# Where a batch's variances stand in VectorE's order: behind the last row maximum of the segment before

## The chip, the cores and the metric

One core of one Trainium2 chip. The metric is the device time of one execution in microseconds, the median of the runs, where lower is better.

## The reference

Two layers over `x` (4 batches x 512 rows x 256) and a context (4 x 1024 x 192). Each layer is a cross attention with 16 heads of 64 followed by a mixture-of-experts block; a layer normalisation without weights stands ahead of each. Cut to what matters here:

```python
def _layernorm(x, axis=-1, eps=1e-05):
    m = jnp.mean(x, axis=axis, keepdims=True)
    v = jnp.var(x, axis=axis, keepdims=True)
    return (x - m) / jnp.sqrt(v + eps)
...
    sim = jnp.einsum('bhid,bhjd->bhij', q, k) * SCALE
    attn = jax.nn.softmax(sim, axis=-1)
    out = jnp.einsum('bhij,bhjd->bhid', attn, v)
...
    x = x + _L0_xattn_ref(_layernorm(x, axis=-1), ctx_768, ...)
    x = x + _L0_ffn_ref(_layernorm(x, axis=-1), ...)
    x = x + _L1_xattn_ref(_layernorm(x, axis=-1), ctx_768, ...)
    x = x + _L1_ffn_ref(_layernorm(x, axis=-1), ...)
```

## The kernel before

The kernel runs four phases one after the other: attention and experts of layer 0, attention and experts of layer 1 (tile names begin with L0a, L0e, L1a, L1e and, for the sorted experts at the end, L1s). The change lies in the two attention phases. They are built by one function, `attention_phase`.

An attention phase is a software pipeline of 32 segments: 4 batches times 8 pairs of heads (`HP = 8`), segment `i` being head pair `i % 8` of batch `i // 8`. Every engine has its own written-out order of instructions for a segment, and the engines are tied by semaphores. In segment `i`

- TensorE transposes the last row maximum (L802), projects the queries of `i + 1`, and forms eight steps `qk(i, p)` of transposed scores (L818, L819), each step pair followed by a part of a value projection (`project_values`, L708); then it projects the output of `i - 1` (L708), and forms the scores of `i + 1` for their row maxima (L796), the products with the values (L833), the keys of `i + 2`, and the sums of the exponentials (L845);
- ScalarE takes the exponentials (L400) and the high parts of keys, weights and values (L381, L371, L375, L464);
- GpSimd (POOL) adds the exponentials over the keys (`psums`, L326), and forms low parts by a subtraction of two operands in SBUF: of the context (L334, in segments 0 and 1 of a batch), of the value weights (L312, in even segments) and of the attention weights (L307, in every segment);
- VectorE (DVE) works in the order `low_keys(i + 1, 1)` (L521, the low parts of the second half of the next keys, two instructions), the layer normalisation's piece of this segment if there is one, `normalise(i - 1)` (L535 reciprocal, L538), `high_output` and `low_output` (L544, L548), the queries' high and low parts (L504, L509), `add_output(i - 1)` (L558), and the four row maxima of `i + 1` (L530), with two instructions of L521 among them.

The normalisation of the batches next door is spread over the segments of a batch by `step = i % 8`: statistics in steps 0 and 1 (L566), the variances in step 2 (`ROOT`), then a square root on ScalarE behind its exponentials (L406), and the scales in steps 3 and 4. `variance` handles 4 or 8 columns (128x4 or 128x8). It issues six small instructions: L578, L579 and L580 follow one another with no wait between them, L581, L582 and L583 each stand behind a wait on a VectorE semaphore (`link`). All but L583 read two operands in SBUF.

A few other instructions that read two operands in SBUF come into the rows below: L624 (VectorE, segment 0) adds the bias to the residual; in the experts' phase L1087 (GpSimd) forms a chunk's low weights, L1181 (VectorE) forms low parts, L1208 follows it with no wait, and L1209 stands behind a wait on L1208's semaphore.

Two waits on TensorE look at VectorE here. In `project_values` the first part in an even segment waits for `low_keys(i + 1, 1)`, whose keys share its bank; the third part waits for `low_output(i - 1)`:

```python
elif n % 2 == 0:
    pe.wait_ge(sem["klo"], 2 * (i + 1) + 2)
...
else:
    pe.wait_ge(sem["olo"], i)
```

Of the kernel before, what the change touches and what calls it, by code (L numbers as in the profile page):

```python
# [46 lines left out]
def build(nc, x, ctx_top, ctx_bot, layer_in, out):  # L47
# [6 lines left out]
    with stack:  # L54
# [37 lines left out]
        def attention_phase(tag, weights, value_weights, bias, xres, prefetch, source=None, again=False, keep=False, clear=()):  # L92

            with scope() as s:
# [29 lines left out]
                with nc.Block() as block:  # L124
# [23 lines left out]
                    def half_of(n):  # L148
                        return slice(n * BANK, (n + 1) * BANK)

                    def bank_of_keys(i, half):
                        return bank(SPARE if i < 2 and half == 0 else PLACE[f"K{half}"])
# [10 lines left out]
                    NEXT_STATS, LAST_STATS, ROOT, INNER, OUTER, BIAS = 0, 1, 2, 3, 4, 7  # L163
# [17 lines left out]
                    def columns_of(b):  # L181

                        used = [column for _, column in batches_of(b)] if b >= 0 else [0]
                        return slice(min(used), max(used) + QT)
# [313 lines left out]
                    def _(dve):  # L498
# [15 lines left out]
                        def low_keys(i, n, heads=(0, 1)):  # L514
                            par, cols = i % 2, half_of(n)
                            if heads == (0,) and n == 0:
                                dve.wait_ge(sem["first_hi"], i + 1)
                            else:
                                dve.wait_ge(sem["hi"], 2 * i + n + 1)
                            for h in heads:  # L520
                                last = nc.vector.tensor_tensor(k_st[HEAD[1 - h], par, h, cols], bank_of_keys(i, n)[HEAD[h], :],  # L521
                                                               k_st[HEAD[h], par, h, cols], ALU.subtract)
                            if 1 in heads:
                                last.then_inc(sem["klo"], 1)
# [8 lines left out]
                        def normalise(i):  # L533
                            dve.wait_ge(sem["total"], i + 1)
                            nc.vector.reciprocal(inv[:, :], bank(PLACE["TOTAL"])).then_inc(sem["inv"], 1)  # L535
                            dve.wait_ge(sem["inv"], i + 1)
                            dve.wait_ge(sem["pv"], i + 1)
                            nc.vector.tensor_tensor(O, O, inv[:, :], ALU.mult).then_inc(sem["norm"], 1)  # L538
# [21 lines left out]
                        def statistics(b, step):  # L560

                            c, column = (b + 1, 0) if step == NEXT_STATS else (b - 1, QT)
                            if step == LAST_STATS:
                                dve.wait_ge(sem["added"], BEFORE + 2 * (b * HP - 1) + 2)
                            for t in range(QT):
                                nc.vector.bn_stats(stats[:, column + t, :], xres[:, c * QT + t, :]).then_inc(sem["stat"], 1)  # L566
                            dve.wait_ge(sem["stat"], counted_stats(b, step))
# [3 lines left out]
                        def link(b, n, ins):  # L571
                            ins.then_inc(sem["link"], 1)
                            dve.wait_ge(sem["link"], LINKS * (b + 1) + n)

                        def variance(b):
                            c = columns_of(b)
                            me, se, mo, so = (stats[:, c, i] for i in (1, 2, 4, 5))
                            nc.vector.tensor_tensor(total_of[:, c], me, mo, ALU.add).then_inc(sem["link"], 1)  # L578
                            nc.vector.tensor_tensor(var[:, c], se, so, ALU.add).then_inc(sem["link"], 1)  # L579
                            link(b, 3, nc.vector.tensor_tensor(dif[:, c], me, mo, ALU.subtract))  # L580
                            link(b, 4, nc.vector.scalar_tensor_tensor(dif[:, c], dif[:, c], DIM / 4.0, dif[:, c], ALU.mult, ALU.mult))  # L581
                            link(b, 5, nc.vector.tensor_tensor(var[:, c], var[:, c], dif[:, c], ALU.add))  # L582
                            nc.vector.tensor_scalar(var[:, c], var[:, c], 1.0 / DIM, EPS, ALU.mult, ALU.add).then_inc(sem["var"], 1)  # L583

                        def inner_scales(b):
                            c = columns_of(b)
                            dve.wait_ge(sem["sqrt"], b + 2)
                            if b > 0:
                                dve.wait_ge(sem["xn"], 2 * len([i for i in GROUPS if i <= b * HP + INNER]) + 2)
                            link(b, 6, nc.vector.reciprocal(rstd[:, c], std[:, c]))  # L590
                            link(b, 7, nc.vector.tensor_tensor(dif[:, c], var[:, c], rstd[:, c], ALU.mult))
                            link(b, 8, nc.vector.tensor_tensor(dif[:, c], dif[:, c], rstd[:, c], ALU.mult))

                        def outer_scales(b):
                            c = columns_of(b)
                            link(b, 9, nc.vector.tensor_scalar(dif[:, c], dif[:, c], -0.5, 1.5, ALU.mult, ALU.add))
                            link(b, 10, nc.vector.tensor_tensor(rstd[:, c], rstd[:, c], dif[:, c], ALU.mult))
                            link(b, 11, nc.vector.scalar_tensor_tensor(shift[:, c], total_of[:, c], -0.5, rstd[:, c], ALU.mult, ALU.mult))
                            dve.sem_inc(sem["scale"], 1)
# [17 lines left out]
                        def add_bias(b):  # L617
                            if b == 0:
                                dve.wait_ge(sem["bias"], 16)
                                dve.wait_ge(sem["xn"], 2)  # L620
                            else:
                                dve.wait_ge(sem["xn"], rows_of(b))
                            rows = xres[:, b * QT:(b + 1) * QT, :]
                            nc.vector.tensor_tensor(rows, rows, bias_sb[:, :].unsqueeze(1).broadcast_to([P, QT, DIM]), ALU.add)\  # L624
                                .then_inc(sem["biased"], 1)

                        def segment(i):
                            if i + 1 < SEGMENTS:
                                low_keys(i + 1, 1)
                            b, step = divmod(i, HP)  # L630
                            if step == NEXT_STATS and b + 1 < BATCH:
                                if b == 0 and source is not None:
                                    dve.wait_ge(sem["x1"], 16)
                                statistics(b, step)
                            if step == LAST_STATS and b > 0:
                                statistics(b, step)
                            if step == ROOT:
                                variance(b)
                            if step == INNER:
                                inner_scales(b)  # L640
                            if step == OUTER:
                                outer_scales(b)
                            if i == 0:
                                add_bias(0)
                            if step == BIAS and b + 1 < BATCH:
                                add_bias(b + 1)
                            if i > 0:
                                normalise(i - 1)
                            if i > 0:
                                high_output(i - 1)  # L650
                                low_output(i - 1)
                            if i + 1 < SEGMENTS:
                                high_queries(i + 1)
                                low_queries(i + 1)
                            if i > 0:
                                if i in GROUPS:
                                    low_rows(number(i), GROUPS[i][0], PLACE["XT"])
                                add_output(i - 1)
                            if i + 1 < SEGMENTS:
                                for qt in range(QT):  # L660
                                    maximum(i + 1, qt)
                                    if qt in (1, 2) and i + 2 < SEGMENTS:
                                        low_keys(i + 2, 0, (qt - 1,))

                        nc.vector.memset(row_max[:, QT - 1, :], 0.0).then_inc(sem["pad"], 1)
                        if source is not None:
# [1097 lines left out]
```

## Time and profile before

| | before |
|---|---|
| median of 3 runs | 2612.82 us (2611.64 to 2613.31) |
| profiled execution, its own time | 2618.82 us |
| its span | 2616.9 us |
| granted TensorE clock, mean over the span | 0.985 |
| TensorE matmul busy | 96% |
| VectorE busy | 80% |
| GpSimd busy | 57% |
| ScalarE busy | 48% |

The profiled execution took 6.0 us more than the median of the timed ones; the span leaves out 1.9 us of it. Positions in the rows below are microseconds from the start of the span.

### The profile page before, as it was taken

Reading aid. Unit: us, or ns where it says so; the run is one execution under the profiler, and the core shown is the slowest. Engines: PE = TensorE matmul, PEld = TensorE weight load, DVE = VectorE, ACT = ScalarE, POOL = GpSimd, SP = SyncE. Lnnn points to the kernel's source line nnn. Section 1 sums busy time; section 2 is a strip of 40 time slices with the busy share of each in tenths; the row PEclk is TensorE's granted clock in tenths of the full one; section 3 lists DMA queues with packets and bytes.
Section 4 is the critical chain, followed back from the end, with each engine's and each line's share of the span. In section 5 each row is a group of like instructions: output and inputs, shape, how many; then the busy total and the mean of one; then the engine's idle time right before and its main releaser. Section 6 shows DMA issues by size and latency. Waiting matters only on the chain. (4 is left out here: it accounts for less than half of the span.)

```text
span 2616.9 us, 37958 instructions
## 1 busy us (share of the span) xinstructions
PE 2520.7 (96%) x13304; PEld 1776.5 (68%) x13304; DVE 2091.2 (80%) x2602; ACT 1246.1 (48%) x1774; POOL 1482.1 (57%) x1124
## 2 busy tenths in 40 slices
PE   8999999999999889999999899999999999998795
PEld 6666565656665678888888766666666665656684
DVE  7888888888888487777777788888888888866695
ACT  5555555555554323333333355455555454533393
POOL 5878777877777311111111187687878777760345
PEclk9999999999999999999999999999999999999897
DMA  4122212222221200000000121222131222115112
GB/s 147 45 59 53 63 45 58 63 49 50 63 51 41 72 19 24 24 24 24 24 24 18 47 75 45 55 61 59 45 79 45 59 53 55 45 29 235 47 54 88
DMA packets 118648, 145.09 MB, mean 55 GB/s; under 512 B 63856, under 2 KB 80112, under 8 KB 117488
## 3 DMA queue, kind: packets, MB, share of 16 engines
q1 hardware_dynamic: 113664, 136.10, 19.3%
q0 software_dynamic: 1536, 4.20, 0.5%
q10 hardware_dynamic: 3312, 3.02, 0.3%
q8 instruction: 81, 1.33, 0.2%
q14 instruction: 55, 0.45, 0.1%
HBM read 80.93 MB, written 11.80 MB: 35 GB/s over the span
## 5 line engine op out<-in xcount | busy, mean ns | idle before, releaser
L326 POOL TENSOR_TENSOR L1a_psums<-L1a_psums,L1a_probs 128x512 f32<-128x512 f32 x384 | 479.1, 1293 | 0.0
L326 POOL TENSOR_TENSOR L0a_psums<-L0a_psums,L0a_probs 128x512 f32<-128x512 f32 x384 | 478.8, 1289 | 0.0
L530 DVE TENSOR_REDUCE L1a_row_max<-psum 128x2 f32<-128x2048 f32 x128 | 293.6, 2293 | 59.2 <-PE psum L796 58.9
L530 DVE TENSOR_REDUCE L0a_row_max<-psum 128x2 f32<-128x2048 f32 x128 | 293.5, 2293 | 57.7 <-PE psum L796 57.2
L400 ACT ACTIVATE L0a_probs<-psum 128x1024 f32<-128x1024 f32 x256 | 251.6, 1027 | 105.9 <-PE psum L819 105.7
L400 ACT ACTIVATE L1a_probs<-psum 128x1024 f32<-128x1024 f32 x256 | 251.6, 1027 | 105.1 <-PE psum L819 104.9
L1168 DVE SCALAR_TENSOR_TENSOR xres<-psum,L0e_weights_of,xres 128x256 f32<-128x256 f32 x544 | 225.6, 478 | 22.6 <-PE psum L1379 21.7
L833 PE MATMUL psum<-L1a_probs,L1a_v 128*64 128x512 f32 x1024 | 240.5, 601 | 0.0
L833 PE MATMUL psum<-L0a_probs,L0a_v 128*64 128x512 f32 x1024 | 240.4, 601 | 0.0
L1365 PE MATMUL psum<-xnT_hi,L0e_w_hi 128*128 128x512 f32 x544 | 215.0, 395 | 9.4 <-DVE L0e_hid L1176 9.4
L1365 PE MATMUL psum<-xnT_lo,L0e_w_hi 128*128 128x512 f32 x544 | 214.6, 394 | 0.0
L1365 PE MATMUL psum<-xnT_hi,L0e_w_lo 128*128 128x512 f32 x544 | 213.1, 392 | 0.0
L818 PE MATMUL psum<-L0a_q_hh,L0a_k_st 128*128 128x512 f32 x512 | 204.4, 399 | 1.4 <-ACT L0a_probs L400 0.9
L818 PE MATMUL psum<-L1a_q_hh,L1a_k_st 128*128 128x512 f32 x512 | 204.3, 399 | 1.4 <-ACT L1a_probs L400 0.9
L819 PE MATMUL psum<-L1a_q_lm,L1a_k_hs 65*128 65x512 f32 x512 | 203.1, 397 | 0.0
L819 PE MATMUL psum<-L0a_q_lm,L0a_k_hs 65*128 65x512 f32 x512 | 203.0, 397 | 0.0
L1113 ACT ACTIVATE L0e_act_g<-psum 128x512 f32<-128x512 f32 x136 | 81.3, 598 | 243.4 <-PE psum L1365 243.4
L558 DVE TENSOR_TENSOR xres<-psum,xres 128x512 f32<-128x512 f32 x128 | 88.6, 692 | 114.9 <-PE psum L708 113.8
L1176 DVE TENSOR_TENSOR L0e_hid<-psum,L0e_act_g 128x512 f32<-128x512 f32 x136 | 93.7, 689 | 102.8 <-ACT L0e_act_g L1113 102.7
L326 POOL TENSOR_TENSOR L1a_psums<-L1a_probs 128x512 f32<-128x512 f32 x64 | 82.4, 1307 | 153.5 <-ACT L1a_probs L400 153.5
L1087 POOL TENSOR_TENSOR L0e_w_lo<-L0e_raw,L0e_w_hi 128x768 fp32r<-128x768 f32 x16 | 30.0, 1875 | 242.1 <-ACT L0e_w_hi L1102 242.1
L1087 POOL TENSOR_TENSOR L0e_w_lo<-ctx_stage,L0e_w_hi 128x768 fp32r<-128x768 f32 x16 | 30.6, 1914 | 240.9 <-ACT L0e_w_hi L1102 240.9
(384 smaller groups left out, 6148.6 us busy)
## 6 DMA issues: line engine op xcount, KB each, us to landing
L0a_k_hs<-L0a_k_st SPq DMA_DIRECT2D x64, 256.0 KB, 3.6
L1a_k_hs<-L1a_k_st SPq DMA_DIRECT2D x64, 256.0 KB, 3.7
L0a_raw<-in_attention SPq DMA_DIRECT2D x33, 384.0 KB, 3.4
L1a_raw<-in_attention SPq DMA_DIRECT2D x33, 384.0 KB, 3.4
L1weights<-in_sorted SPq DMA_DIRECT2D x2, 6144.0 KB, 20.6
L0a_q_hh<-L0a_q_hh SPq DMA_DIRECT2D x64, 128.0 KB, 2.3
L1a_q_hh<-L1a_q_hh SPq DMA_DIRECT2D x64, 128.0 KB, 2.3
ctx_stage<-in_experts SPq DMA_DIRECT2D x19, 384.0 KB, 3.0
```

The lines of the kernel that those rows point to most:

```text
L326: nc.gpsimd.tensor_tensor(psums[:, h, :], a, probs[:, h, kv, :], ALU.add).then_inc(sem["acc"], 1)
L400: nc.scalar.activation(probs[:, h, 2 * kp:2 * kp + 2, :], slot(h).rearrange("p (n q) -> p n q", n=2), ACT.Exp, scale=SCALE)\
L530: nc.vector.reduce_max(row_max[:, qt, 0:33:32], psum[:, 0:4 * BANK].rearrange("p (h k) -> p h k", h=2), axis=AX.X).then_inc(sem["max"], 1)
L558: nc.vector.tensor_tensor(rows, bank(PLACE[f"OUT{half}"]), rows, ALU.add).then_inc(sem["added"], 1)
L818: nc.tensor.matmul(dst, k_st[:, par, h, keys_of], q_hh[:, par, h, :], start=True, stop=False)
L819: last = nc.tensor.matmul(dst, k_hs[0:DH + 1, par, h, keys_of], q_lm[0:DH + 1, par, h, :], start=False, stop=True)
L833: last = nc.tensor.matmul(O[HEAD[h], :], v[:, pair % 2, kv, cols], probs[:, h, kv, :], start=kv == 0, stop=kv == KVT - 1)
L1087: nc.gpsimd.tensor_tensor(w_lo[:, par, :], raw[par], w_hi[:, par, :], ALU.subtract)\
L1113: nc.scalar.activation(act_g[:, u % 2, :], bank(u % 2), ACT.Silu).then_inc(sem["silu"], 1)
L1168: last = nc.vector.scalar_tensor_tensor(acc, bank(4 + 2 * (u % 2) + n // 2)[:, (n % 2) * DIM:(n % 2 + 1) * DIM], weights_of[:, ds(j * (2 * ...
L1176: nc.vector.tensor_tensor(hid[:, u % 2, :], bank(2 + u % 2), act_g[:, u % 2, :], ALU.mult)\
L1365: last = nc.tensor.matmul(bank(2 * g + u % 2), a[:, par, w], m[:, kd, rows], start=n == 0, stop=n == 3 * KD - 1)
```

## The change

The call of `variance(b)` is moved up in VectorE's order: from segment `8b + 2`, where it stood behind the low keys (L521) and ahead of the reciprocal (L535), to the end of segment `8b + 1`, behind the fourth row maximum (L530) and so ahead of those low keys. Nothing else moves, no wait is added or taken away, and no other engine's order changes. The variances of the first batch before the pipeline starts, `variance(-1)`, stay where they are.

```diff
@@ -634,8 +634,6 @@
                                 statistics(b, step)
                             if step == LAST_STATS and b > 0:
                                 statistics(b, step)
-                            if step == ROOT:
-                                variance(b)
                             if step == INNER:
                                 inner_scales(b)
                             if step == OUTER:
@@ -661,6 +659,8 @@
                                     maximum(i + 1, qt)
                                     if qt in (1, 2) and i + 2 < SEGMENTS:
                                         low_keys(i + 2, 0, (qt - 1,))
+                            if step + 1 == ROOT:
+                                variance(b)
```

## Rows read from the trace of the kernel before

**Rows 1.** The page's first part: busy time, share of span, instructions.

```profile
PE 2520.7 (96%) x13304; PEld 1776.5 (68%) x13304; DVE 2091.2 (80%) x2602; ACT 1246.1 (48%) x1774; POOL 1482.1 (57%) x1124
```

**Rows 2.** Windows: seven segments with variances, first, last, sum; then the segments before.

```profile
86.00:113.00 27.00, 26.50 (x136) 16.32 (x134) 23.50 (x25) 15.55 (x21) 21.86 (x17) 1.00 0.26 65
...
1984.42:2011.49 27.07, 26.51 (x136) 16.30 (x134) 23.57 (x25) 15.56 (x21) 21.93 (x17) 1.00 0.26 65
sum 189.30, PE 185.60 PEld 114.20 DVE 164.79 ACT 108.91 POOL 153.26; mean PE 26.51 PEld 16.32 DVE 23.54 ACT 15.56 POOL 21.89
...
sum 183.67, PE 183.67 PEld 114.57 DVE 156.74 ACT 98.39 POOL 148.44; mean PE 26.24 PEld 16.37 DVE 22.39 ACT 14.06 POOL 21.21
```

**Rows 3.** Timeline of VectorE: start, duration, instruction; layer 0, segment 10.

```profile
294.94 2.29 DVE L530 TENSOR_REDUCE L0a_row_max<-psum 128x2 f32<-128x2048 f32 x1 [0.37 <-PE psum L796]
297.26 1.39 DVE L521 TENSOR_TENSOR L0a_k_st<-psum,L0a_k_st 64x512 fp32r<-64x512 f32 x2
298.69 1.49 DVE L578 TENSOR_TENSOR L0a_total_of<-L0a_stats 128x8 f32<-128x8 f32 x1
...
300.18 0.16 DVE L580 TENSOR_TENSOR L0a_dif<-L0a_stats 128x8 f32<-128x8 f32 x1
300.37 0.17 DVE L581 SCALAR_TENSOR_TENSOR L0a_dif<-L0a_dif 128x8 f32<-128x8 f32 x1
...
300.98 3.36 DVE L535 RECIPROCAL L0a_inv<-psum 128x512 f32<-128x512 f32 x1
...
305.83 0.69 DVE L548 TENSOR_TENSOR L0a_o_split<-psum,L0a_o_split 128x512 fp32r<-128x512 f32 x1
```

**Rows 4.** Timeline of GpSimd around the same place, and its next L307.

```profile
297.07 1.28 POOL L312 TENSOR_TENSOR L0a_wv<-L0a_raw_v,L0a_wv 128x512 fp32r<-128x512 f32 x1
298.30 1.84 POOL L307 TENSOR_TENSOR L0a_w_split<-L0a_raw,L0a_w_split 128x768 fp32r<-128x768 f32 x1
301.32 1.29 POOL L326 TENSOR_TENSOR L0a_psums<-L0a_probs 128x512 f32<-128x512 f32 x1 [1.17 <-ACT L0a_probs L400]
...
320.18 1.82 POOL L307 TENSOR_TENSOR L0a_w_split<-L0a_raw,L0a_w_split 128x768 fp32r<-128x768 f32 x1 [1.39 <-ACT L0a_w_split L371]
```

**Rows 5.** Timeline of TensorE and its weight loads in the same segment.

```profile
300.72 0.42 PEld L708 LDWEIGHTS psum<-L0a_wv,ctx_hi 128*128 128x128 f32 x2
...
305.65 0.39 PE L819 MATMUL psum<-L0a_q_lm,L0a_k_hs 65*128 65x512 f32 x1
...
306.58 0.30 PEld L708 LDWEIGHTS psum<-L0a_wv,ctx_hi 128*128 128x128 f32 x2 [0.97 <-DVE L0a_o_split L548]
```

**Rows 6.** The eighth place (layer 1, segment 26): VectorE, GpSimd and the window.

```profile
2198.03 0.17 DVE L578 TENSOR_TENSOR L1a_total_of<-L1a_stats 128x4 f32<-128x4 f32 x1
...
2198.97 3.36 DVE L535 RECIPROCAL L1a_inv<-psum 128x512 f32<-128x512 f32 x1
...
2194.20 1.82 POOL L307 TENSOR_TENSOR L1a_w_split<-L1a_raw,L1a_w_split 128x768 fp32r<-128x768 f32 x1
...
2196.90:2223.14 26.24, 26.24 (x135) 16.38 (x133) 22.20 (x25) 15.57 (x21) 19.31 (x15) 1.00 0.24 58
```

**Rows 7.** Timeline, segment 0 of layer 0: a VectorE instruction behind GpSimd's.

```profile
38.00 1.29 POOL L326 TENSOR_TENSOR L0a_psums<-L0a_probs 128x512 f32<-128x512 f32 x1 [1.71 <-ACT L0a_probs L400]
...
39.24 2.27 POOL L326 TENSOR_TENSOR L0a_psums<-L0a_probs 128x512 f32<-128x512 f32 x1
...
38.47 1.90 DVE L624 TENSOR_TENSOR xres<-xres,L0a_bias_sb 128x1024 f32<-128x1024 f32 x1
```

**Rows 8.** Timeline, experts of layer 0: a GpSimd instruction behind VectorE's.

```profile
929.69 2.98 POOL L1087 TENSOR_TENSOR L0e_w_lo<-ctx_stage,L0e_w_hi 128x768 fp32r<-128x768 f32 x1 [19.34 <-ACT L0e_w_hi L1102]
...
929.69 0.69 DVE L1181 TENSOR_TENSOR L0e_hid_lo<-L0e_hid,L0e_hid_hi 128x512 fp32r<-128x512 f32 x1
930.29 0.69 DVE L1208 TENSOR_TENSOR L0e_gt<-L0e_choice,L0e_late 128x512 f32<-128x512 f32 x1
931.02 2.20 DVE L1209 TENSOR_TENSOR L0e_eq<-L0e_choice,L0e_late 128x512 f32<-128x512 f32 x1
```

## The prediction

> **What bounds the kernel now.** The page's first part comes first: TensorE's matmuls are busy 96% of the span [rows 1]. So an edit on VectorE counts only where TensorE waits for VectorE. For that I cut the attention phases into segments at TensorE's transpose of the last row maximum and asked for windows. Seven of the eight segments that hold the variances last 27.00 to 27.13 us, 189.30 us in sum; the seven segments just ahead of them last 183.67 us in sum [rows 2]. The difference, 5.63 us or 0.80 us a segment, is what the variances cost now. It is also the most that moving them can give back.
>
> VectorE's timeline of one such segment shows how it comes about [rows 3]. From the variances' first instruction to the reciprocal they take 300.98 − 298.69 = 2.29 us, of which L578 alone is 1.49 us, though it has 8 columns. At the eighth place the same instruction takes 0.17 us and the whole 0.94 us [rows 6]. GpSimd's timeline tells them apart [rows 4, 6]: in the seven, L307 runs from 298.30 to 300.14 and L578 ends 0.04 us behind it, at 300.18; in the eighth L307 was over at 2196.02, 2.0 us ahead of L578. L578 and L307 both read two operands in SBUF, and VectorE stands until GpSimd is done.
>
> Last comes TensorE's timeline [rows 5]. Its last L819 ahead of the value projection starts at 305.65, and the next weight load only at 306.58, released by L548, which ends at 306.52 [rows 3]. That is the stall. Where the variances took 0.94 us the segment lasted 26.24 us, with no stall [rows 6]. So what counts is when L535, and with it L548, comes: 2.29 us of variances cost 0.80 us, the first 1.49 us are free.
>
> **The change, part by part.** The six instructions remain and nothing is waited for anew, but they stand 1.43 us earlier (L521 to L578 now, 297.26 to 298.69 [rows 3]), and GpSimd is then inside another pair of instructions. Their price at the new place is no row of the trace. I work it out at the segment of rows 3; the other six repeat it within a few hundredths.
>
> *Removed:* 2.29 us between L521 and L535.
>
> *Added ahead of L521:* L530 ends at 294.94 + 2.29 = 297.23. L578 has no wait in front of it, so it is issued between 297.15 (with no wait between, L1208 started 0.09 us before L1181 ended [rows 8]) and 297.26. GpSimd's L312 runs from 297.07 to 298.35, and L307 is queued right behind it, from 298.30 [rows 4]. I need to know who gets through when both queue.
> - A VectorE instruction that waits behind one of GpSimd's goes ahead of GpSimd's next. L624 was issued at 38.47 inside L326 (38.00 to 39.29) and ended at 40.37; the second L326, issued at 39.24, took 2.27 us for the 1.29 us of the first [rows 7]. So L578 goes ahead of L307 and ends 0.04 us behind L312, at 298.39.
> - VectorE instructions with no wait between them keep GpSimd out, and a wait between them lets it in. L1181 and L1208 ran back to back, 929.69 to 930.98, while L1087 stood; L1087 then ended at 932.67, 1.69 us after them, and L1209, behind a wait of only 0.04 us, took 2.20 us for the 0.69 us of L1208 [rows 8]. L579 and L580 have no wait in front, L581 has one. So L580 ends 0.16 us after L578 (as now, 300.34 after 300.18 [rows 3]), at 298.55, and then L307 goes in. It has the shape of L1087 and ends 1.69 us later, at 300.24.
> - L581 ends 0.04 us behind it, at 300.28. GpSimd has nothing more queued, since its L326 waits for the exponentials until 301.32 [rows 4]. From the end of L581 to the next instruction is 0.44 us (300.54 to 300.98 [rows 3]): L521 starts at 300.72.
>
> So VectorE spends 300.72 − 297.26 = 3.46 us on the variances and not 2.29. Behind them L521 and its gap take 1.43 us as before, and L535 starts at 302.15 where it started at 300.98: 1.17 us later. The move carries the chain across one GpSimd instruction more: it waits for the rest of L312, and then for all of L307 in its middle.
>
> *What is late next.* L521 now ends near 302.11. The value projection behind it would load its weights at 300.72 [rows 5], so TensorE stands there for about 1.4 us, a stall that did not exist (L521 ended at 298.65, 2.1 us early). With this it reaches the second wait about 1.3 us later, while L548 ends 1.17 us later, at 307.69: it stands there again, about half a microsecond in place of 0.93. Both waits hang on one VectorE chain, so they don't add: the segment ends later by the shift of L548 alone, 1.17 us.
>
> *What hides the rest.* GpSimd's L312 and L307 end up to 0.1 us later; the 1.17 us of idle time behind them covers it [rows 4]. Its next additions need the exponentials behind the first stall and slip by 1.3 us; they had 1.39 us to spare before the next L307, whose own input also comes later with TensorE [rows 4]. The square root is taken at the end of ScalarE's segment, so variances ready earlier or later are worth nothing there. No DMA waits for the low keys.
>
> *The eighth place:* GpSimd is idle, the variances take 0.94 us again, L521 ends 0.94 us later inside its 2.1 us of slack: nothing.
>
> *The sum:* 7 × 1.17 = 8.2 us. Both ends of the unknown, the order of access: if L307 went ahead of L578, L578 would end at 300.18 and L521 start at 300.98, 1.43 us late, 10.0 us in all; if L578, issued at 297.15, got in before L312 (issued only 0.08 us ahead of it), L312 would end near 298.6, L307 near 300.4 with L582 behind it, and L521 would start near 300.67: 1.12 us, 7.8 us in all. On the profiled execution's own time: 2618.8 + 8.2 = 2627.0, a factor of 1.0031; on the median, 2612.8 × 1.0031 = **2621.0 us**.
>
> The Trainium skill (SBUF — State Buffer, Who interferes with whom) says the shared port pair is an exclusive lock for the whole instruction, and that issue order decides who blocks. The rows agree that one side stands entirely. Taken to the letter, issue order would put L307 (298.30) ahead of L579 (298.31), which rows 8 speak against; it is the second rival.
>
> **Rivals.**
> 1. *VectorE keeps the access through its short waits* (not slower). The waits between L580 and L583 are 0.03 us each; if GpSimd doesn't get in there, the chain ends 298.39 − 300.18 + 300.98 = 299.19, L535 starts at 300.62, 0.36 us earlier than now, and the stall shrinks to 0.44 us a segment: −2.5 us, 2610.3. It decides wherever L307 can't start within a gap of 0.03 us. For it: L307 is one instruction's processing away from running. Against it: L1087 got in at a gap of 0.04 us [rows 8]. The floor under it, with all stalls gone, is −5.6 us, 2607.2 [rows 2]. Chance 0.12 with the floor.
> 2. *GpSimd's queued L307 goes in earlier.* Ahead of L579, L307 ends at 298.39 + 1.69 = 300.08, and L579 to L583 follow as now: L521 at 300.84, 1.29 us late, 9.0 us, 2621.8. Ahead of L578: 10.0 us, 2622.8. For it: L307 starts 0.05 us before L312 ends, back to back. Against it: rows 7, where the second L326 did the same and lost. Chance 0.10.
> 3. *The shift is taken up by slack I don't see,* as the statistics of steps 0 and 1 are in their segments (26.24 us on average just ahead [rows 2]): under 4 us, near 2615. Against it: beyond 1.49 us every tenth of the variances showed in the segment now. Chance 0.05.
>
> **How the numbers follow.** The forecast (7.8 to 8.2 us, either order at L312) has 0.73; its own range is 2619 to 2623, from the 1.7 us between the runs of before. With rival 2 it is 0.83, which reaches to 2622.8 and with the same spread to 2625. At the low end a shift of half a microsecond a segment, partly covered, gives 2616.5. Range 2616.5 to 2625. A measurement of this kernel tells 0.2%, 5.2 us, from no change. The forecast and rival 2 lie over it; of their 0.83 I give 0.05 to a time just under it. Rivals 1 and 3 are within it, but for 0.03 at the floor. Faster 0.03, same 0.19, slower 0.78.
>
> **What would show it.** Right: L578 of about 1.1 to 1.2 us right behind L530, L581 (or L582) of about 1.7 to 1.9 us, L307 of about 2 us on GpSimd; TensorE's weight load at the first part of the value projection released by L521, 1.4 us late; seven segments of 28.2 us and the eighth of 26.24. Wrong: L581 and L582 at 0.17 us each with L307 pushed behind L583, and segments of 26.7; or L578 at 2.9 us, with the order of rival 2. What would make it wrong altogether is a GpSimd that starts L312 somewhere else than some 0.1 us ahead of L578.

## The result, and the profile after

The changed kernel takes 2620.76 us (median of 8 runs, 2616.93 to 2621.79), the kernel before 2612.28 us (8 runs, 2611.32 to 2614.47): a ratio of 1.0029 with a 95% interval of 1.0018 to 1.0040. The medians lie 8.5 us apart, the ratio makes it 7.6 us. The kernel is slower, by an amount that the measurement can tell from nothing.

The windows after, cut like [rows 2] at the transpose of the last row maximum (start:end and length, then busy time and instructions of TensorE, its weight loads, VectorE, ScalarE and GpSimd, the granted clock, DMA's share and GB/s). The first of the seven is shown, then the eighth place, and the sum is that of the seven:

```profile
86.48:114.77 28.29, 26.74 (x135) 16.25 (x133) 24.80 (x25) 15.54 (x21) 21.89 (x17) 1.00 0.24 62
...
2206.56:2232.80 26.24, 26.24 (x135) 16.38 (x134) 22.20 (x23) 15.56 (x21) 19.31 (x15) 1.00 0.24 58
...
sum 198.13, PE 187.19 PEld 113.65 DVE 173.69 ACT 108.74 POOL 153.35; mean PE 26.74 PEld 16.24 DVE 24.81 ACT 15.53 POOL 21.91
```

The seven segments last 198.13 us where they lasted 189.30 [rows 2]: 8.83 us more, 1.26 us each. The eighth has 26.24 us as before [rows 6]. Every other segment of the two attention phases lasts as long in both kernels to within 0.05 us (26.1 to 26.7 us, the last one 25.4), so all of the difference that the attention phases make is in the seven. The granted clock is 1.00 in them, TensorE's upper level of 2.4 GHz, so the clock has no part in it.

VectorE's timeline in the segment of [rows 3] shows what they are made of (start, duration, instruction, then idle time before it with its releaser):

```profile
296.71 2.29 DVE L530 TENSOR_REDUCE L0a_row_max<-psum 128x2 f32<-128x2048 f32 x1 [0.37 <-PE psum L796]
299.04 1.11 DVE L578 TENSOR_TENSOR L0a_total_of<-L0a_stats 128x8 f32<-128x8 f32 x1
300.07 0.16 DVE L579 TENSOR_TENSOR L0a_var<-L0a_stats 128x8 f32<-128x8 f32 x1
300.15 1.82 DVE L580 TENSOR_TENSOR L0a_dif<-L0a_stats 128x8 f32<-128x8 f32 x1
302.01 0.17 DVE L581 SCALAR_TENSOR_TENSOR L0a_dif<-L0a_dif 128x8 f32<-128x8 f32 x1
...
302.61 1.39 DVE L521 TENSOR_TENSOR L0a_k_st<-psum,L0a_k_st 64x512 fp32r<-64x512 f32 x2
304.03 3.36 DVE L535 RECIPROCAL L0a_inv<-psum 128x512 f32<-128x512 f32 x1
...
308.88 0.69 DVE L548 TENSOR_TENSOR L0a_o_split<-psum,L0a_o_split 128x512 fp32r<-128x512 f32 x1
```

And GpSimd's, in the same place:

```profile
298.84 1.28 POOL L312 TENSOR_TENSOR L0a_wv<-L0a_raw_v,L0a_wv 128x512 fp32r<-128x512 f32 x1
300.08 1.87 POOL L307 TENSOR_TENSOR L0a_w_split<-L0a_raw,L0a_w_split 128x768 fp32r<-128x768 f32 x1
303.09 2.51 POOL L326 TENSOR_TENSOR L0a_psums<-L0a_probs 128x512 f32<-128x512 f32 x2 [1.15 <-ACT L0a_probs L400]
307.06 14.97 POOL L326 TENSOR_TENSOR L0a_psums<-L0a_psums,L0a_probs 128x512 f32<-128x512 f32 x12 [1.46 <-ACT L0a_probs L400]
323.19 1.82 POOL L307 TENSOR_TENSOR L0a_w_split<-L0a_raw,L0a_w_split 128x768 fp32r<-128x768 f32 x1 [1.16 <-ACT L0a_w_split L371]
```

Read the ends against each other. L312 ends at 300.12 and L578 at 300.15. L307 ends at 301.95 and L580 at 301.97. Two of the six instructions stand until the GpSimd instruction beside them is over; the other four take 0.16 or 0.17 us. The other six places repeat this within 0.02 us. From L578's start to L521's it is 302.61 − 299.04 = 3.57 us. Before, the six took 2.29 us in their old place [rows 3]. TensorE's timeline shows who pays:

```profile
304.15 0.47 PE L708 MATMUL psum<-L0a_wv,ctx_hi 128*128 128x256 f32 x2 [1.27 <-DVE L0a_k_st L521]
...
309.63 0.51 PE L708 MATMUL psum<-L0a_wv,ctx_hi 128*128 128x256 f32 x2 [0.32 <-DVE L0a_o_split L548]
...
304.12 0.30 PEld L708 LDWEIGHTS psum<-L0a_wv,ctx_hi 128*128 128x128 f32 x2 [1.67 <-issue]
...
309.63 0.30 PEld L708 LDWEIGHTS psum<-L0a_wv,ctx_hi 128*128 128x128 f32 x2 [0.74 <-DVE L0a_o_split L548]
```

Before there was one stall in the segment, behind L548 [rows 5]. Now there is one behind L521 first, and the old one is shorter. Behind L521 the trace names L521 at the matmul only; at the weight load, which waits 1.67 us, it names no releaser ("issue"). The trace's list of waits (engine and line, released by, us in total, times, longest) has the new one in all seven segments, four in layer 0 and three in layer 1:

```profile
PE psum L708 <- DVE L0a_k_st L521: 5.0, 4, 1.3
...
PE psum L708 <- DVE L1a_k_st L521: 3.8, 3, 1.3
```

### The profile page after: what moved, and what is told of

It reads as the page before. It is cut to its first block and busy times, and to the rows that moved or that the text cites. A ratio compares the mean times of both kernels' runs of the same rounds, so it can differ in the third digit from the quotient of the medians.

```text
span 2619.1 us, 37958 instructions
## 1 busy us (share of the span) xinstructions
PE 2516.0 (96%) x13304; PEld 1771.1 (68%) x13304; DVE 2100.4 (80%) x2602; ACT 1246.0 (48%) x1774; POOL 1482.4 (57%) x1124
## 5 line engine op out<-in xcount | busy, mean ns | idle before, releaser
L326 POOL TENSOR_TENSOR L0a_psums<-L0a_psums,L0a_probs 128x512 f32<-128x512 f32 x384 | 478.9, 1289 | 5.8 <-ACT L0a_probs L400 5.8
L326 POOL TENSOR_TENSOR L1a_psums<-L1a_psums,L1a_probs 128x512 f32<-128x512 f32 x384 | 478.9, 1289 | 4.3 <-ACT L1a_probs L400 4.3
L530 DVE TENSOR_REDUCE L0a_row_max<-psum 128x2 f32<-128x2048 f32 x128 | 293.6, 2293 | 57.7 <-PE psum L796 57.4
L530 DVE TENSOR_REDUCE L1a_row_max<-psum 128x2 f32<-128x2048 f32 x128 | 293.5, 2293 | 57.7 <-PE psum L796 57.4
L326 POOL TENSOR_TENSOR L1a_psums<-L1a_probs 128x512 f32<-128x512 f32 x64 | 82.3, 1305 | 153.5 <-ACT L1a_probs L400 153.5
```

Of the source, the lines that this page charges most:

```text
L326: nc.gpsimd.tensor_tensor(psums[:, h, :], a, probs[:, h, kv, :], ALU.add).then_inc(sem["acc"], 1)
L530: nc.vector.reduce_max(row_max[:, qt, 0:33:32], psum[:, 0:4 * BANK].rearrange("p (h k) -> p h k", h=2), axis=AX.X).then_inc(sem["max"], 1)
```

## The experiments

Theory A: the whole price, before and after, is waiting for GpSimd. L578 waits for L312, one more of the six waits for L307, and without these waits the place of the variances costs nothing. Theory B: the new place has a price of its own, since it puts the six ahead of the low keys, L521, for which TensorE's value projection waits. Two questions on the order of access were still open too: who goes first when both engines queue, and whether all GpSimd work is alike.

Of each run, the ratio is to the kernel before, run beside it, whose median was 2615.67 us (30 runs) beside experiments 1 to 4 and 2613.11 us (15 runs) beside 5 and 6. So a ratio or a count of segments can be compared between runs, a bare time can't. "Segments" is the length of the seven segments in its profile, and their excess is the sum over 7 × 26.24 = 183.68 us. By that count the kernel before has 5.6 us of excess and the changed one 14.4.

| kernel | ratio (95% interval) | segments, us | excess, us | less before's 5.6, us | by the ratio, us |
|---|---|---|---|---|---|
| the changed kernel | 1.0029 (1.0018 to 1.0040) | 28.28 to 28.32 | 14.4 | +8.8 | +7.6 |
| 1: GpSimd behind the variances | 0.9974 (0.9963 to 0.9984) | 26.24 | 0.0 | −5.6 | −6.8 |
| 2: only L307 behind them | 0.9986 (0.9977 to 0.9995) | 26.62 to 26.67 | 2.8 | −2.8 | −3.7 |
| 3: split between both places | 0.9996 (0.9987 to 1.0005) | 26.86 to 26.90 | 4.5 | −1.1 | −1.0 |
| 4: old place, segment 3 | 0.9983 (0.9974 to 0.9992) | 26.24 | 0.0 | −5.6 | −4.4 |
| 5: old place, GpSimd behind | 0.9980 (0.9971 to 0.9989) | 26.47 to 26.53 | 2.0 | −3.6 | −5.2 |
| 6: under the additions | 1.0231 (1.0215 to 1.0247) | 32.3 to 37.5 (all eight) | 66.5 | +60.9 | +60.4 |

(The last column is the ratio less one times 2612 to 2616 us. Runs 5 and 6 have something at the eighth place as well; it is in their excess.) The last two columns differ by 1.6 us at most, which is inside every interval. The segments leave out the rest of the program, which no version changes: what lies outside the two attention phases took between 970.0 and 976.6 us in the eight profiled executions. So the segments can be read finer than the medians, and what a version is worth is what its segments say.

**1. GpSimd's two instructions held until the variances are done.** Against the changed kernel. The place of the change stays; L312 and L307 can't be beside the six.

```
 def segment(i):
+    if i % HP == ROOT:
+        pool.wait_ge(sem["var"], i // HP + 2)
     if i % 2 == 0 and i // 2 + 1 < PAIRS:
         low_values(i // 2 + 1)
```

> The changed order, with GpSimd told to wait for the variances before its L312 and L307 of that segment (one wait more, in segments 8b+2). Theory A (the price is GpSimd's access, not the place): no variance instruction is held up, the six take 0.94 us as at the eighth place, which is under the 1.49 us that are free; L312 then runs from about 1.0 us after the last row maximum, L307 ends just ahead of the next L326, and all seven segments last 26.24 us: 5.6 us under before, near 2606.7, and 14 us under the changed kernel. Theory B (the place ahead of the low keys costs, whoever uses the access): the low keys are still behind the variances, TensorE still stands at the value projection, and the time stays above before, 2615 to 2620.

Measured: 2608.60 us (8 runs), ratio 0.9974. VectorE in the same segment (L580 to L585 are the changed kernel's L578 to L583, L523 its L521):

```profile
296.29 0.17 DVE L580 TENSOR_TENSOR L0a_total_of<-L0a_stats 128x8 f32<-128x8 f32 x1
296.38 0.17 DVE L581 TENSOR_TENSOR L0a_var<-L0a_stats 128x8 f32<-128x8 f32 x1
...
297.27 1.39 DVE L523 TENSOR_TENSOR L0a_k_st<-psum,L0a_k_st 64x512 fp32r<-64x512 f32 x2
```

The six take 0.98 us in place of 3.57, in the same place on VectorE, and the windows of all seven segments are those of a segment with nothing in it:

```profile
296.58:322.82 26.24, 26.24 (x135) 16.38 (x133) 22.23 (x23) 15.57 (x21) 22.35 (x17) 1.00 0.26 68
...
sum 183.69, PE 183.69 PEld 114.65 DVE 155.54 ACT 109.00 POOL 156.37; mean PE 26.24 PEld 16.38 DVE 22.22 ACT 15.57 POOL 22.34
```

TensorE is busy in every microsecond of them. So the 14.4 us of the changed kernel are waits for GpSimd and nothing else. For the 5.6 us of the kernel before, whose six stand in another place, it takes experiments 4 and 5. GpSimd's L328 (the L326 of before) now starts with no idle time at 300.44: the delay used up its 1.15 us of spare time and cost nothing more.

**2. Only L307 held.** The same wait, placed between `low_values` and `low_weights`: L312 stays beside the six.

> As the run before, but only L307 waits for the variances; L312 stays where it is. Theory A: L578 is held up by L312 (1.1 us) and nothing behind it is; the six take 1.9 to 2.0 us in place of 3.57, the segments last 26.7 us, 2.5 us under before, near 2609.8. So L312 would be worth 0.4 us and L307 1.6 us a segment. Theory B: as in the run before, 2615 to 2620.

Measured: 2611.75 us (11 runs), ratio 0.9986.

```profile
295.54 1.10 DVE L580 TENSOR_TENSOR L0a_total_of<-L0a_stats 128x8 f32<-128x8 f32 x1
296.56 0.16 DVE L581 TENSOR_TENSOR L0a_var<-L0a_stats 128x8 f32<-128x8 f32 x1
296.64 0.17 DVE L582 TENSOR_TENSOR L0a_dif<-L0a_stats 128x8 f32<-128x8 f32 x1
...
297.45 1.39 DVE L523 TENSOR_TENSOR L0a_k_st<-psum,L0a_k_st 64x512 fp32r<-64x512 f32 x2
```

L578's wait for L312 is still there, 1.10 us, and the instruction that took 1.82 us takes 0.17. Of the 14.4 us, L312 alone makes 2.8 (0.40 us a segment), and L307 adds the other 11.6 (1.66 us). The 1.65 us by which L580 is longer than 0.17 reach the end whole, since L312's delay has used up the free time. The shares hold in this order only: the free time goes to whichever delay is counted first, and no run has L307 beside the six in the new place without L312.

**3. Split.** Against the kernel before: part 0 of `variance` is L578 and L579, in the new place; part 1 is the other four, in the old one. L307 then runs beside L521, which reads PSUM and one operand in SBUF.

```
 if step == ROOT:
-    variance(b)
+    variance(b, 1)
...
+if step + 1 == ROOT:
+    variance(b, 0)
```

> Only L578 and L579 at the new place, the other four at the old one, behind the low keys L521, which have one operand in SBUF. Theory A: L578 takes 1.1 us behind L312, L307 runs under L521, and L580 is held up for only 0.3 us: L535 comes 0.1 to 0.2 us earlier than before, segments 26.9 us, near 2611.3. Theory B: the low keys are late by 1.2 us of their 2.1 us of slack and VectorE does the same work: about as before or, if the low keys' lateness costs in proportion, 2615.

Measured: 2613.53 us (11 runs), ratio 0.9996, which can't be told from the kernel before; segments 26.86 to 26.90 us against its 27.00 to 27.13. GpSimd's instruction and VectorE's stand here one below the other (L579 and L580 are the changed kernel's L578 and L579, and L583 is its L580):

```profile
297.63 1.87 POOL L307 TENSOR_TENSOR L0a_w_split<-L0a_raw,L0a_w_split 128x768 fp32r<-128x768 f32 x1
...
296.60 1.10 DVE L579 TENSOR_TENSOR L0a_total_of<-L0a_stats 128x8 f32<-128x8 f32 x1
297.62 0.16 DVE L580 TENSOR_TENSOR L0a_var<-L0a_stats 128x8 f32<-128x8 f32 x1
297.81 1.39 DVE L521 TENSOR_TENSOR L0a_k_st<-psum,L0a_k_st 64x512 fp32r<-64x512 f32 x2
299.24 0.29 DVE L583 TENSOR_TENSOR L0a_dif<-L0a_stats 128x8 f32<-128x8 f32 x1
```

L521 takes its usual 1.39 us under L307: it isn't held. Only the last 0.26 us of L307 (to 299.50) meet an instruction with two operands in SBUF, and that one takes 0.29 us in place of 0.17. The waits are a matter of which instruction lies beside which, not of GpSimd being busy. From L579 to L521 the first two and their gap take 1.21 us (296.60 to 297.81) and the other four 0.93 us (299.24 to 300.17), 2.14 us in all.

**4. The old place, one segment later.** The kernel before with `ROOT` 3 in place of 2, and the inner scales moved from step 3 to 4. GpSimd prepares value weights in even segments alone, and its L307 there is over before the six come.

> The kernel before with ROOT = 3 and INNER = OUTER = 4: the variances behind the low keys of segment 8b+3, the square root at the end of that segment, and both pieces of the scales in segment 8b+4. GpSimd has nothing to run there (its L307 is over 3 us ahead and the next additions come 2 us later). Theory A: variances 0.94 us, scales about 1.3 us, both under the 1.49 us that are free: all segments 26.24 us, near 2606.7. Theory B says nothing of this place. A third possibility is that the scales in one piece (six instructions, 1.2 to 1.3 us) go over the free time and give back some tenths a segment, 2608 to 2610.

Measured: 2609.99 us (11 runs), ratio 0.9983. All segments last 26.24 us, and the six take 0.16 to 0.17 us each. The scales in one piece take 1.35 us (353.12 to 354.47), less than the 1.49 us that are free, so the third possibility didn't come about either. The same 5.6 us come back without a wait on GpSimd. That speaks against theory B's counterpart as well: the old place isn't bad either, only what lay beside it.

**5. The old place with experiment 1's wait.** If the new place has no price of its own, this is as fast as experiment 1.

> The order of before (variances behind the low keys), with GpSimd told to wait for them ahead of L312 and L307, as in e1_pool_after_var. Theory A (access alone): the variances take 0.94 us here too, all segments last 26.24 us, 5.6 us under before, the same as e1_pool_after_var. GpSimd's additions start 1.5 us later than before and have 1.4 us to spare, so at most 0.1 us a segment could come back. Theory B (the place ahead of the low keys has a price of its own): this one is faster than e1_pool_after_var.

Measured: 2608.20 us (11 runs), ratio 0.9980. The variances are uncontended, 0.98 us from L580's start to the reciprocal's, but the segments last 26.47 to 26.53 us, and 26.42 at the eighth place. TensorE's weight loads name the cause:

```profile
300.37 0.30 PEld L710 LDWEIGHTS psum<-L0a_wv,ctx_hi 128*128 128x128 f32 x2 [0.43 <-POOL L0a_wv L312]
```

and GpSimd's rows the rest:

```profile
299.03 1.29 POOL L312 TENSOR_TENSOR L0a_wv<-L0a_raw_v,L0a_wv 128x512 fp32r<-128x512 f32 x1 [2.76 <-issue]
300.28 1.84 POOL L307 TENSOR_TENSOR L0a_w_split<-L0a_raw,L0a_w_split 128x768 fp32r<-128x768 f32 x1
```

L312 makes the low value weights that the value projection loads. Held behind the variances of the old place it ends at 300.32, and TensorE wants them some 0.4 us earlier. In experiment 1 L312 starts 0.79 us into its segment (297.37 − 296.58) and here 2.22 us (299.03 − 296.81), so there it is over in time. The expectation said that at most 0.1 us a segment would be left; it was 0.23 to 0.29, and 0.18 at the eighth place. It missed a user of GpSimd's result that isn't GpSimd. By segments the new place is better than the old by 2.0 us once GpSimd waits, and the medians can't tell them apart. Theory B is refuted: the place that it blames is the better one.

**6. The six under GpSimd's long series.** Against the kernel before. The variances moved to the segment ahead, behind the low queries and ahead of `add_output`, where GpSimd runs twelve of its additions, L326, back to back. It asks what the order of access does when GpSimd never pauses.

```
-    if step == ROOT:
-        variance(b)
...
         high_queries(i + 1)
         low_queries(i + 1)
+    if step + 1 == ROOT:
+        variance(b)
     if i > 0:
```

> The variances in segment 8b+1 ahead of add_output (L558), where VectorE is idle for 1.4 us but GpSimd runs its additions L326 back to back, one every 1.25 us. Theory A with what the changed kernel showed (a queued GpSimd instruction goes in behind the second variance instruction and then at every wait): L578 is held up by the rest of one L326, and L580, L581 and L582 each by a whole one; the six take about 4.5 us, L558 comes 3 us late in all eight places, and the 5.6 us of before are given back: plus 18 us, near 2631; if L583, with one operand in SBUF, is held up as well, plus 28 us, near 2641. The weaker reading (GpSimd gets in once for the whole group): the six take 2.6 us, L558 is 1.1 us late, plus 3 us, near 2615. Theory B: TensorE doesn't wait for anything here, and the idle time hides them: 2607.

Measured: 2672.71 us (4 runs), ratio 1.0231, far over both expectations. VectorE, at the segment of the rows above and at the next place:

```profile
287.53 0.45 DVE L578 TENSOR_TENSOR L0a_total_of<-L0a_stats 128x8 f32<-128x8 f32 x1
287.91 1.33 DVE L579 TENSOR_TENSOR L0a_var<-L0a_stats 128x8 f32<-128x8 f32 x1
289.16 1.31 DVE L580 TENSOR_TENSOR L0a_dif<-L0a_stats 128x8 f32<-128x8 f32 x1
290.50 1.18 DVE L581 SCALAR_TENSOR_TENSOR L0a_dif<-L0a_dif 128x8 f32<-128x8 f32 x1
291.72 1.19 DVE L582 TENSOR_TENSOR L0a_var<-L0a_var,L0a_dif 128x8 f32<-128x8 f32 x1
292.94 1.19 DVE L583 TENSOR_SCALAR L0a_var<-L0a_var 128x8 f32<-128x8 f32 x1
...
506.76 10.29 DVE L578 TENSOR_TENSOR L0a_total_of<-L0a_stats 128x8 f32<-128x8 f32 x1
```

```profile
282.91 14.86 POOL L326 TENSOR_TENSOR L0a_psums<-L0a_psums,L0a_probs 128x512 f32<-128x512 f32 x12
...
502.14 14.88 POOL L326 TENSOR_TENSOR L0a_psums<-L0a_psums,L0a_probs 128x512 f32<-128x512 f32 x12
```

In the first case L578 waits for the rest of one addition and each of the other five for a whole one, 1.2 to 1.3 us, with or without a wait of its own in front: 6.6 us for what takes 0.94 alone. In the second L578 is let in only when the series ends (517.02; L578 ends at 517.05), having waited through the rest of one addition and all of the next eight. That happened at two of the eight places (the other is 2231.02, 10.28 us). At a third, L578 took 2.95 us, the rest of one and two more; at the other five it took 0.45 to 0.65 us. GpSimd's series takes 14.86 and 14.88 us for its twelve, against 14.97 without the six beside it (the changed kernel's row above), so VectorE pays all of it.

The delay costs TensorE more than its own length. It waits for the first row maximum behind the six, and then runs for a while at a lower clock:

```profile
297.71 1.22 PE L796 MATMUL psum<-L0a_k_st,L0a_q_hh 64*128 64x512 f32 x4 [4.71 <-DVE L0a_row_max L530]
```

```profile
276.65:310.46 33.81, 29.10 (x136) 18.10 (x134) 29.14 (x29) 14.05 (x19) 21.36 (x17) 0.90 0.19 50
298.00:304.00 6.00, 6.00 (x16) 3.85 (x16) 2.98 (x2) 1.65 (x3) 0.00 (x0) 0.50 0.07 3
304.00:308.00 4.00, 4.00 (x22) 1.27 (x20) 3.15 (x3) 3.02 (x5) 0.80 (x1) 1.00 0.52 131
```

The stall ends at 297.71. The granted clock (third number from the end) is 0.50 of full speed from 298 to 304, the lower of the two levels, 1.2 GHz, and 1.00 again from 304 on. Over the segment it is 0.90, where the same segment has 1.00 in the kernel before and in the changed one. Of the 33.81 − 26.24 = 7.57 us that this segment lost, 4.71 are the stall. The other 2.9 us agree with TensorE's busy time, which is 2.86 us more than the 26.24 of a full segment for as many instructions. The windows of all eight segments, added up, say the same:

```profile
sum 276.38, PE 229.69 PEld 143.09 DVE 242.09 ACT 111.44 POOL 169.25; mean PE 28.71 PEld 17.89 DVE 30.26 ACT 13.93 POOL 21.16
```

They lost 66.5 us, of which 276.38 − 229.69 = 46.7 us are stalls, and 229.69 − 8 × 26.24 = 19.8 us are matmuls that took longer. The granted clock is 0.86 to 0.90 in each of the eight.

## Why the prediction was right

Forecast were 2621.0 us and a shift of 8.2 us; measured were 2620.76 and 8.5 between medians, 8.8 by segments. The sign and the mechanism held; the order of access in the middle of the six did not. That the two times agree to 0.3 us is in part luck: the forecast's shift is 0.6 us too small by segments, and the median of the kernel before came out 0.5 us lower, over eight runs, than the one that the forecast started from.

- **L578 goes ahead of L307 and ends behind L312.** Right: 1.10 to 1.11 us, 0.03 us behind L312's end. Experiment 2 isolates it: 1.10 us with L307 gone.
- **L578 to L580 keep GpSimd out, L307 goes in behind L580, and L581 is held.** Wrong. L307 went in behind L579, with no semaphore wait between L579 and L580, and L580 was held. It is the same at all seven places. This is a variant that rival 2 priced, 1.29 us a segment and 9.0 us in all, except that L307 went ahead of L580 and not of L579. The step that failed is the rule drawn from [rows 8], that instructions with no wait between them keep GpSimd out. It cost little, because whichever of the six is held, the six wait for L307 once. Rival 2's order gives 3.58 us for the six, 300.84 − 297.26, which is nearer to the measured 3.57 than the forecast's 3.46.
- **The six take 3.46 us.** Measured 3.57. L307 ended 1.72 us behind L579 (301.95 − 300.23), where 1.69 us was taken from the experts of layer 0, and three instructions were left behind it and the held one where the forecast had two. The shift that reaches L548 is 1.28 us in place of 1.17: L548 starts 12.17 us behind L530's start, where it was 10.89 [rows 3]. This is the term that was too small, by 0.11 us × 7 = 0.8 us.
- **Segments of 28.2 us, the eighth 26.24.** Right: 28.28 to 28.32, and 26.24.
- **A new stall of about 1.4 us behind L521, a second of about half a microsecond behind L548, and the two don't add.** Right in kind. Counted from L530's start, the first weight load of the value projection comes 7.41 us on and not 5.78, 1.63 us later; the matmuls stand 1.27 us. The second load comes 12.92 us on and not 11.64 [rows 3, 5]: 1.28 us later, the shift of L548 and no more. At that place the load waits 0.74 us where it waited 0.97. The half microsecond forecast doesn't follow from the forecast's own terms, which give 0.93 + 1.17 − 1.3 = 0.8 us. The slip is without effect, since the sum goes by the shift of L548.
- **GpSimd's later work hides its own delay.** Right: its additions waited 1.46 us once more for the exponentials, and the L307 behind them still had 1.16 us of idle time, from 1.39. Experiment 1 delays GpSimd further and costs nothing, and experiment 5 shows where that ends: at L312, when its own result comes late.
- **The first 1.49 us of the variances are free.** Right, and not only in the old place. Whatever VectorE spends on the six ahead of L535, less 1.49 us, is what the segment gets longer: 1.91 us in experiment 2 (297.45 − 295.54) gives 0.42, measured 0.38 to 0.43; 2.14 us in experiment 3 gives 0.65, measured 0.62 to 0.66; 3.57 us in the changed kernel gives 2.08, measured 2.04 to 2.08; 0.98 us in experiment 1 gives nothing, measured nothing. So it makes no difference whether the time is spent ahead of L521 or behind it, which is what theory B denied. Experiment 5 is the exception, by another chain, that of L312.
- **From the profiled execution to the median.** The forecast for the profiled execution was 2627.0 us, and it took 2620.84. The profiled execution of before was itself 6.5 us over the median (2618.82 against 2612.28), and that of after was not. The summary of TensorE's transposes L802 shows where they differ; first of before, then of after:

```profile
L802 PE MATMUL psum<-ident,L0a_row_max x32: 269/298/298, 33.6 to 854.1; 128*33 128x128 f32 x32
L802 PE MATMUL psum<-ident,L1a_row_max x32: 269/298/298, 1507.9 to 2327.7; 128*33 128x128 f32 x32
```

```profile
L802 PE MATMUL psum<-ident,L0a_row_max x32: 269/298/298, 34.1 to 859.7; 128*33 128x128 f32 x32
L802 PE MATMUL psum<-ident,L1a_row_max x32: 269/297/298, 1513.9 to 2337.4; 128*33 128x128 f32 x32
```

Layer 0's attention is longer by 825.6 − 820.5 = 5.1 us, four segments of 1.26; layer 1's by 823.5 − 819.8 = 3.7 us, three of them. At 2337.4 the changed kernel is 9.7 us behind, yet its span is only 2.2 us longer. The missing 7.5 us lie behind the attention of layer 1, in code that the change doesn't touch. From that last transpose to the end of the span it was 289.2 us in the execution of before and 281.7 in that of after; in the profiled executions of the six experiments it was 282.8 to 286.8. So the one was the longest of the eight and the other the shortest, and why they differ is open. Scaling the median, and not taking the profiled execution's time as the start, kept this out of the forecast.

Rival 1 (VectorE keeps the access through its short waits) and rival 3 (slack takes it up) are both refuted by the held L580 and by seven equal segments. The floor that rival 1 named, −5.6 us, is real. Experiments 1 and 4 reach it, with the change's place and with the old one.

What stays open: what decides the order when both engines queue. Small reads that are over at once may let GpSimd in between L579 and L580, where the 128x512 operands of L1181 and L1208 kept it out [rows 8]; this is argued, and no run changed the size of an operand. Nor is it known why L578 got in ahead of the next addition at five places of experiment 6 and not at the other three. The moment isn't what tells them apart: at 287.53, where it got in, and at 506.76, where it didn't, it came 0.87 us behind the start of an addition (286.66 and 505.89).

## What to carry to other kernels

Before an instruction is moved on one of two engines that share access to SBUF, lay the other engine's timeline beside the new place: its price there is set by what lies beside it, not by its size (0.17 us alone, up to 10.3 here). In this kernel a handful of small instructions with two SBUF operands was best put where the other engine is idle. Making the other engine wait for them did as well where it had slack, but only where nobody wanted its result sooner. Where a stall moves to a wait further up the same chain, count the shift of the chain's last link, not the stalls.

## What the runs showed of the hardware

- **The order of access isn't fixed, and a waiting instruction can be passed over again and again.** In every place of the changed kernel L578 went in between L312 and L307, as L624 did before [rows 7]. In experiment 6 a VectorE instruction issued at 506.76 stood 10.29 us, while eight GpSimd instructions went ahead that were all issued after it. The Trainium skill (SBUF — State Buffer, Who interferes with whom) says that the one that issues first gets the shared ports for its whole instruction and the other blocks fully. The full block is what the traces show. The changed kernel agrees with the order of issue too: L579 (300.07) went ahead of L307 (300.08), and L307 ahead of L580 (300.15). But 0.01 us proves little: in experiment 6 L580 was issued at 289.16 and an addition at 289.17, and the addition went first. The 10.29 us contradict the order of issue outright.
- **A gap isn't needed for GpSimd to get in.** L307 came between L579 and L580, which start 0.08 us apart and have no wait between them.
- **One SBUF operand can be enough.** In experiment 6 L583, a tensor-scalar instruction of fp32 on 128x8 elements in SBUF, was held like its neighbours, 1.19 us in place of 0.17. L521, with one operand in PSUM, was not: 1.39 us under L307 as without it. The same section of the Trainium skill counts the tensor-scalar form among those that can enter a mode which uses both port pairs; this row agrees with that, at a size of 8 columns.
- **A stall that costs more than itself.** In experiment 6 the six took 5.7 us longer than alone (6.64 us for 0.94) and cost the segment 7.6 us: a stall of 4.71 us, and 2.9 us because TensorE ran the 6 us behind it at a granted clock of 0.50. The stalls of up to 1.27 us in the changed kernel left it at 1.00.
